# An own issue order for three pipeline slots, a last group mixed and stored in halves, and a swapped copy and shift, in a four-layer graph network

## The chip, the cores and the metric

One core of one Trainium2 chip runs the kernel. The time is device microseconds of one execution; lower is better. The kernel before has a median of 635.74 us over three runs (634.36 to 636.84).

## The reference

64 graphs of 128 nodes with 128 features pass through four layers. Each layer takes `h = relu(layernorm(x))` and adds its result to x:

```
x = x + attention(h, adj)        # 4 heads: leaky relu of e_i + e_j, masked by adj, softmax over neighbours
x = x + mlp((1 + eps) h + adj h) # 128 -> 256 -> 128, biases
x = x + adj (h W) + b            # graph convolution
x = x + gru(h, adj) * nodemask   # 5 steps: m = h W_l; agg = A^T m; h = gru_cell(agg, h)
```

All weights are inputs, and so are the biases, x, adj and the mask. The output is x, in float32.

## The kernel before, in words

Graphs are taken in groups of four (`GROUP`), so an operation has 512 columns on 128 partitions; there are 16 groups. Everything stays in SBUF from the first load to the last store. Five programs, one for each engine, are written out by hand; what orders them is the order of calls in each engine's `slot` function and semaphores between them.

**First layers.** `first_layers` runs a software pipeline of 19 slots. In slot `number`, `at(back)` is group `number - back`: the scores and softmax of `at(2)`, the attention product of `at(3)`, layer 1 of `at(4)`, layer 2 of `at(5)`, the layer norm ahead of the recurrent layer for `at(6)` and `at(7)`. The same functions are called in every slot, with exceptions for the first ones. The functions that matter here:

- Softmax of a group: TensorE adds the mask (`mask`) and the scores (`scores`) in four PSUM banks, ScalarE rectifies each graph's (`leaky`, L1132), VectorE takes the row maxima (`row_max`, L1327), GpSimd subtracts them (`less_max`, L720), ScalarE exponentiates (`exponential`, L1137), TensorE transposes (`turn_prob`, L878), and ScalarE and VectorE copy two graphs each to SBUF (`keep_probT`, L1142 and L1331).
- Attention: TensorE multiplies and sums (`attend`, `sum_up`), VectorE copies, divides and adds to x (`keep_attended`, `divide`, `add_attended`, L1354; signal `x_attended`). `mask` of graph 3 waits for `x_attended` of the group before, since it reuses its bank.
- Layer 1: VectorE computes `shift = -mean * rstd` (`shift_of`, L1302), ScalarE normalises (`normalise`, L1101), GpSimd adds (1 + eps) I to the transposed adjacency (`add_self`, L707), TensorE multiplies (`neighbours`, `hidden`, `out_0`).
- Layer 0: GpSimd centres and scales the next group (`centre`, L729; `scale`, L736), TensorE transposes it (`turn_y0`), ScalarE copies it (`keep_hT`, L1110). `centre` waits for the transpose of the group before.
- `GruWeights` fuses the five W_l with the input weights on TensorE (`turn`, `fuse`), copies the products on ScalarE (`keep`, `keep_fused`, L261) and derives a power-of-two scale from their largest magnitude on VectorE (`row_max` to `scaled_biases`). The recurrent layer first needs it in slot 18.

**Recurrent layer.** `gru_layer` takes 80 steps of four interleaved groups, with a tail in which pipeline slots 80 to 83 drain. For each step TensorE multiplies state parts and gathered parts by the gate weights (`gate`), ScalarE applies sigmoids and tanh (L1720, L1722, L1728, L1733), VectorE combines (L1779, L1788, L1792), GpSimd multiplies z by the state and adds the new state (L1745, L1751). A group that has ended is transposed back (`back`, L1668), masked and added to x (`finish`, L1766), and stored in one transfer (`store`, L1811).

Of the kernel before, what the change touches and what calls it, by code (L numbers as in the profile page):

```python
# [144 lines left out]
class GruWeights:  # L145
# [7 lines left out]
    def __init__(self, nc, io, t, psum, ctx, until_gru):  # L153
# [9 lines left out]
        self.fused_banks = [B_SUM, B_EDGE, B_SUM, B_EDGE, B_SUM]  # L163
# [48 lines left out]
    def turn(self, pe, lot):  # L212
# [5 lines left out]
        elif lot == 1:  # L218
            pe.wait_ge(self.wi_loaded, 16)
            pe.wait_ge(self.kept, 1)  # L220
            bank, sources = self.bank, [gw[:, 4, :], wi[:, 0, :], wi[:, 1, :], wi[:, 2, :]]
        elif lot == 2:
            pe.wait_ge(self.wh_loaded, 16)
            pe.wait_ge(self.kept, 2)
            bank, sources = self.bank, [wh[:, 0, :], wh[:, 1, :], wh[:, 2, :]]
# [9 lines left out]
    def keep(self, act, lot):  # L235
# [7 lines left out]
        elif lot == 2:  # L243
            last = a.copy(self.gf[:, GRU_STEPS, :], bank[:, 0:384])
# [4 lines left out]
    def fuse(self, pe, l):  # L249

        if l == 0:
            pe.wait_ge(self.kept, 3)
        elif l > 1:
            pe.wait_ge(self.fused_kept, l - 1)
# [15 lines left out]
    def all_rows_max(self, dve):  # L270

        dve.wait_ge(self.maxed, 3)
        self.nc.vector.tensor_reduce(self.top[:, 0:1], self.tops[:, :], AXIS.X, ALU.max).then_inc(self.maxed, 1)

    def turn_max(self, pe):
        pe.wait_ge(self.maxed, 4)
# [3 lines left out]
    def whole_max(self, dve):  # L280
# [3 lines left out]
        dve.wait_ge(self.maxed, 5)  # L284
        v.tensor_scalar(self.top1[:, 0:1], self.top1[:, 1:2], LEAST, None, ALU.max).then_inc(self.maxed, 1)

    def spread_max(self, pe):

        pe.wait_ge(self.maxed, 6)
# [187 lines left out]
LAYERS = range(4)  # L477

# [57 lines left out]
def first_layers(nc, io, t, psum, tiles, gru, score_weights, recurrent, ctx):  # L536
# [38 lines left out]
    shifted = sem("shifted")  # L575
    exp_done = sem("exp_done")
# [123 lines left out]
    def gpsimd(pool):  # L700
# [115 lines left out]
    def tensor(pe):  # L816
# [42 lines left out]
        def scores(group):  # L859

            pe.wait_ge(e_lo, group.count)
            for g in range(GROUP):
# [3 lines left out]
            for h in range(HEADS):  # L866
                for g in range(GROUP):
# [77 lines left out]
        def slot(at, number):  # L945
# [12 lines left out]
            if number == 4:  # L958
                pe.wait_ge(gru.fused_kept, 4)
            if at(2) and number > 2:  # L960
                score_terms(at(2))
            if number == 3:
                turn_adj(at(3))
            if at(3):
                attend(at(3), 1)
                sum_up(at(3))
            if number == 3:
                gru.turn(pe, 1)
            if number == 4:
                pe.wait_ge(gru.layers_loaded, gru.all_layers_loaded)  # L970
            if number == 5:
                pe.wait_ge(gru.kept, 4)
            if number == 7:
                pe.wait_ge(gru.maxed, 6)
            if number == 8:
                pe.wait_ge(gru.link, 2)
            if at(4):
                neighbours(at(4), 0, B_SUM, adjT1[at(4).odd], adjT1_ready,
                           (hid_ready[1], at(4).before(1)), (z_ready[0], at(4).before(1)))
            if at(3):  # L980
                turn_attended(at(3))
                turn_sums(at(3))
# [3 lines left out]
            if number == 3:  # L986
                gru.turn(pe, 2)
            if at(4):
# [3 lines left out]
            if at(2) and number > 2:  # L992
                mask(at(2), 2)
                mask(at(2), 3)
# [4 lines left out]
            if at(2):  # L999
                scores(at(2))  # L1000
            if at(5):
                neighbours(at(5), 1, B_EDGE, adjT[at(5).odd], adjT_ready,
                           (e_lo, at(5).before(-3)), (x_added[1], at(5).before(1)), (z_ready[1], at(5).before(1)))
            if number == 2:
                project(at(2))
                turn_y0(at(1))
                gru.turn(pe, 0)
            if number == 3:
                project(at(2))
                gru.fuse(pe, 0)  # L1010
                gru.fuse(pe, 1)
                gru.fuse(pe, 2)
            if number == 4:
                pe.wait_ge(hid_ready[1], 1)
                gru.fuse(pe, 4)
            if at(4):
                out_0(at(4))
            if number == 4:
                pe.wait_ge(gru.fused_kept, 5)
                gru.turn(pe, 3)  # L1020
            if number == 6:
                pe.wait_ge(hid_ready[1], 3)
                gru.turn_max(pe)
            if number == 7:
                pe.wait_ge(hid_ready[1], 4)
                gru.spread_max(pe)
# [6 lines left out]
            if number == 3:  # L1033
                turn_y0(at(1))
# [4 lines left out]
            if number == 3:  # L1039
                gru.fuse(pe, 3)  # L1040
            if at(1) and number > 3:
                turn_y0(at(1))
            if at(2):
                turn_prob(at(2), 2)
                turn_prob(at(2), 3)
            if number == 1:
# [38 lines left out]
    def scalar(act):  # L1085
# [49 lines left out]
        def exponential(group, g):  # L1135
            act.wait_ge(shifted, group.graph_count(g))
# [15 lines left out]
        def slot(at, number):  # L1152
            if number == 0:
                score_weights.pick_rows(act)
            if at(3) and number > 3:
# [12 lines left out]
            if at(2):  # L1168
                keep_e(at(2))
            if at(6):  # L1170
# [5 lines left out]
            if number == 3:  # L1176
                keep_adjT(at(3))
                gru.keep(act, 1)
                gru.keep(act, 2)
            if at(5):  # L1180
                normalise(at(5), 2)
            if at(4):
                keep_hidden(at(4), 0, B_TURN)
                keep_hidden(at(4), 1, B_SUM)
            if at(2):
# [3 lines left out]
                leaky(at(2), 3)  # L1189
            if at(5):  # L1190
                keep_z(at(5), 1, B_EDGE)
            if number == 2:
                keep_hT(at(1))
                gru.keep(act, 0)
            if number == 3:
                gru.keep_fused(act, 0)
                gru.keep_fused(act, 1)
            if number == 4:
                gru.keep_fused(act, 4)
            if at(3):  # L1200
# [5 lines left out]
            if at(2):  # L1206
                exponential(at(2), 0)
            if at(3) and number > 3:
                keep_adjT(at(3))
            if number == 2:  # L1210
                keep_hW(at(2))
            if at(2):
                exponential(at(2), 1)
            if number == 3:
                gru.keep_fused(act, 2)
            if number == 4:
                gru.keep(act, 3)
            if at(2) and number > 2:
                keep_probT(at(2), 0)
            if number == 3:  # L1220
                keep_hT(at(1))
# [5 lines left out]
            if at(1) and number > 3:  # L1227
# [42 lines left out]
    def vector(dve):  # L1270
# [57 lines left out]

        def keep_probT(group, g):
# [33 lines left out]
        def slot(at, number):  # L1363
            if number == 7:
                gru.whole_max(dve)
            if number == 8:
# [5 lines left out]
            if at(3):  # L1372
                keep_probT(at(3), 3)
# [4 lines left out]
            if at(2) and number > 2:  # L1378
                find_gone(at(2))
            if at(3):  # L1380
# [4 lines left out]
            if at(2):  # L1385
# [4 lines left out]
            if at(2):  # L1390
# [3 lines left out]
            if at(3):  # L1394
# [11 lines left out]
            if number == 8:  # L1406
# [3 lines left out]
            if number == 8:  # L1410
                gru.scale_bits(dve)
            if at(2):
                row_max(at(2), 3)
            if number == 4:
                gru.row_max(dve, 2, 4)
            if number == 5:
                gru.row_max(dve, 4, 6)
                gru.all_rows_max(dve)
            if number == 1:
# [3 lines left out]
                score_weights.scale(dve)  # L1423
            if at(4):
                add_out(at(4), 0, B_TURN)
            if number == 8:
                gru.scales(dve)
            if at(0):
                moments(at(0), 0, x_loaded[at(0).odd], at(0).loads)
            if number == 3:  # L1430
                gru.row_max(dve, 0, 2)
            if number == 0:
                score_weights.row_max(dve)
            if at(4) and number < 18:
                moments(at(4), 2, x_added[0], at(4).count)
            if number == 8:
                gru.scaled_biases(dve)
            if at(2):
                keep_probT(at(2), 1)
            if at(5):  # L1440
# [46 lines left out]
def gru_layer(nc, io, t, psum, first, weights, ctx):  # L1487
# [45 lines left out]
    out_ready = sem("out_ready")  # L1533
    stored = [sem(f"stored{s}") for s in range(STREAMS)]

    P = psum[:, :, :, :].rearrange("p s b c -> p (s b) c")
    R, Z, N, T, BACK = [0, 0], [2, 3], [1, 1], [7, 4], 5
    gb = t["gates_b"]
# [36 lines left out]

    def ended_before(j, back):
        return ended_at(j - back)
# [62 lines left out]
    def tensor(pe, remaining):  # L1640
# [30 lines left out]

        def slot(at, s, ended, j):
# [9 lines left out]
            if ended is not None:  # L1682
# [15 lines left out]
            remaining(j)  # L1698
            if here:
# [47 lines left out]

# [102 lines left out]
```

## Time and profile before

| what | us |
| --- | --- |
| median of 3 runs | 635.74 |
| lowest, highest | 634.36, 636.84 |
| the profiled execution | 636.28 |
| its span, first to last instruction | 634.4 |
| TensorE busy | 607.7 (96%) |
| ScalarE busy | 553.2 (87%) |
| VectorE busy | 525.4 (83%) |
| GpSimd busy | 402.3 (63%) |

The span is 1.88 us shorter than the execution it belongs to. Busy shares are averages over two stages with different work: the first layers up to about 260 us, the recurrent layer after them. TensorE's busy time is modelled for pipelined products. The mean granted TensorE clock was 0.995 of full speed.

### The profile page before, as it was taken

The numbers are of one execution on the slowest core, as the hardware profiler recorded it, in microseconds if no ns is written. First come the engines' busy times: TensorE is split into PE (matmuls) and PEld (weight loads), VectorE is DVE, ScalarE is ACT, GpSimd is POOL, SyncE is SP. The second block draws the span as 40 slices with busy tenths as digits, with TensorE's granted clock in tenths as the row PEclk, the third lists the DMA queues.
The fourth block names the chain that finished last, engine by engine and source line by source line (L and its number), as shares of the span: only waits on it lengthen the run. The fifth ranks groups of instructions, "written<-read, shape, count | busy, mean of one in ns | idle before, by whom it ended". The sixth has DMA issues, their size and how long they took to land. (4 is left out here: it accounts for less than half of the span.)

```text
span 634.4 us, 14614 instructions
## 1 busy us (share of the span) xinstructions
PE 607.7 (96%) x5070; PEld 387.2 (61%) x5070; DVE 525.4 (83%) x1312; ACT 553.2 (87%) x1042; POOL 402.3 (63%) x361
## 2 busy tenths in 40 slices
PE   5899999999999999999999999999999999999994
PEld 3567778788888887556545455555555555554552
DVE  6678898988888888889979888888788787787875
ACT  4688899999999999787988888898988889888883
POOL 3456777778877877367577656555565655555564
PEclk9999999999999999999999999999999999999998
DMA  8101011111100000224322324334243423335332
GB/s 182 49 4 54 18 48 32 52 40 33 52 20 18 19 19 1 51 51 62 57 50 51 67 51 85 71 78 80 56 83 67 84 56 80 67 68 84 70 81 67
DMA packets 113643, 35.79 MB, mean 56 GB/s; under 512 B 86625, under 2 KB 113570, under 8 KB 113570
## 3 DMA queue, kind: packets, MB, share of 16 engines
q1 hardware_dynamic: 113424, 34.79, 26.4%
q8 instruction: 41, 0.67, 0.4%
q14 instruction: 32, 0.26, 0.1%
q10 hardware_dynamic: 146, 0.07, 0.0%
HBM read 9.67 MB, written 4.19 MB: 22 GB/s over the span
## 5 line engine op out<-in xcount | busy, mean ns | idle before, releaser
L53 PE MATMUL psum<-h_parts,gru_w 128*128 128x512 f16 x720 | 182.5, 379 | 1.0 <-DVE r L1792 0.8
L53 PE MATMUL psum<-t_parts,gru_w 128*128 128x512 f16 x720 | 181.5, 379 | 0.0
L1751 POOL TENSOR_TENSOR h0T<-r,zh 128x512 f32<-128x512 f32 x80 | 101.6, 1270 | 107.2 <-DVE r L1788 107.1
L1745 POOL TENSOR_TENSOR zh<-z,h0T 128x512 f32<-128x512 f32 x80 | 103.9, 1299 | 34.2 <-ACT z L1720 33.8
L53 PEld LDWEIGHTS psum<-h_parts,gru_w 128*128 128x128 f16 x720 | 69.8, 98 | 82.7 <-DVE r L1792 4.2
L53 PEld LDWEIGHTS psum<-t_parts,gru_w 128*128 128x128 f16 x720 | 66.8, 98 | 66.5 <-DVE t_parts L1775 1.7
L1633 DVE TENSOR_TENSOR h_parts<-h0T,h_parts 128x512 f16<-128x512 f32 x80 | 65.1, 813 | 38.9 <-ACT h_parts L1620 38.7
L1717 ACT CAST t_parts<-psum 128x512 f16<-128x512 f32 x80 | 46.8, 585 | 35.8 <-PE psum L53 35.8
L720 POOL TENSOR_TENSOR prob<-prob,row_max 128x512 f32<-128x512 f32 x64 | 64.5, 1040 | 10.9 <-DVE row_max L1327 10.4
L1775 DVE TENSOR_TENSOR t_parts<-psum,t_parts 128x512 f16<-128x512 f32 x80 | 55.1, 689 | 18.9 <-ACT t_parts L1717 16.6
L1720 ACT ACTIVATE z<-psum,gates_b 128x512 f32<-128x512 f32 x80 | 62.2, 778 | 5.7 <-PE psum L53 0.9
L1728 ACT ACTIVATE r<-r,gates_b 128x512 f32<-128x512 f32 x80 | 65.5, 819 | 0.1
L1792 DVE SCALAR_TENSOR_TENSOR r<-psum,gates_b,r 128x512 f32<-128x512 f32 x80 | 59.8, 747 | 4.4 <-ACT r L1733 4.3
L1733 ACT ACTIVATE r<-psum,gates_b 128x512 f32<-128x512 f32 x80 | 61.6, 770 | 1.7 <-PE psum L53 1.7
L1788 DVE TENSOR_TENSOR r<-r,zc 128x512 f32<-128x512 f32 x80 | 60.1, 751 | 2.8 <-ACT r L1728 2.7
L729 POOL TENSOR_TENSOR y<-x_all,mean_var 128x512 f32<-128x512 f32 x31 | 33.3, 1076 | 44.6 <-DVE mean_var L1285 27.6
L1722 ACT ACTIVATE zc<-psum,gates_b 128x512 f32<-128x512 f32 x80 | 61.5, 769 | 0.0
L1101 ACT ACTIVATE y<-x_all,shift,rstd 128x128 f32<-128x128 f32 x128 | 52.7, 488 | 5.1 <-DVE shift L1302 5.1
L1277 DVE BATCH_NORM_STATS2 stats<-x_all 128x6 f32<-128x128 f32 x256 | 54.9, 276 | 1.9 <-DMA x_all<-in_x 1.5
L53 PEld LDWEIGHTS psum<-edges,h_nodes 128*128 128x128 f16 x640 | 42.3, 98 | 20.7 <-issue 2.3
L1779 DVE TENSOR_TENSOR r<-psum,r 128x512 f32<-128x512 f32 x80 | 54.4, 680 | 0.0
L714 POOL TENSOR_TENSOR x_all<-x_all,b 128x512 f32<-128x512 f32 x32 | 40.7, 1273 | 17.2 <-ACT y L1101 14.7
(148 smaller groups left out, 1126.1 us busy)
## 6 DMA issues: line engine op xcount, KB each, us to landing
x_all<-in_x SPq DMA_DIRECT2D x16, 256.0 KB, 3.8
adj<-in_adj SPq DMA_DIRECT2D x16, 256.0 KB, 3.0
out_x<-y SPq DMA_DIRECT2D x14, 256.0 KB, 2.5
h_nodes<-h_parts SPq DMA_TRANSPOSE x80, 3.1
out_x<-zT SPq DMA_DIRECT2D x2, 256.0 KB, 2.3
gw<-in_L_gnn_weight SPq DMA_DIRECT2D x1, 320.0 KB, 5.4
W<-in_L_gnn_W SPq DMA_DIRECT2D x2, 128.0 KB, 3.1
wi<-in_L_gnn_w_ih SPq DMA_DIRECT2D x1, 192.0 KB, 5.5
```

What stands on the lines that cost most here:

```text
L53: return nc.tensor.matmul(out, lhsT, rhs, start=start, stop=stop)
L720: pool.tensor_tensor(prob[:, g, :, :], prob[:, g, :, :], top[:, g, :].unsqueeze(2).to_broadcast([128, HEADS, NODES]), ALU.subtract).then_i ...
L1633: v.tensor_tensor(by_graph(hp[now.s][:, 1, :]), state(now), by_graph(hp[now.s][:, 0, :]), ALU.subtract)\
L1720: a.activation(z[one.s][:, :], one.Z, ACT.Sigmoid, bias=col(B_Z), scale=col(UNSCALE))\
L1722: a.activation(zc[one.s][:, :], one.Z, ACT.Sigmoid, bias=col(B_NZ), scale=col(N_UNSCALE))\
L1728: a.activation(r[one.s][:, :], r[one.s][:, :], ACT.Tanh, bias=col(B_IN), scale=col(UNSCALE))\
L1733: a.activation(r[here.s][:, :], here.R, ACT.Sigmoid, bias=col(B_R), scale=col(UNSCALE))\
L1745: pool.tensor_tensor(by_graph(zh[now.s][:, :]), by_graph(z[now.s][:, :]), state(now), ALU.mult)\
L1751: pool.tensor_tensor(state(now), by_graph(r[now.s][:, :]), by_graph(zh[now.s][:, :]), ALU.add)\
L1775: v.tensor_tensor(tp[one.s][:, 1, :], one.T, tp[one.s][:, 0, :], ALU.subtract).then_inc(t_lo, 1)
L1788: v.tensor_tensor(r[two.s][:, :], r[two.s][:, :], zc[two.s][:, :], ALU.mult).then_inc(mixed, 1)
L1792: v.scalar_tensor_tensor(r[one.s][:, :], one.N, col(B_HN), r[one.s][:, :], ALU.add, ALU.mult)\
```

## The change

1. **Slots 2 to 4 get an order of their own**, on TensorE, ScalarE, VectorE and GpSimd. In slot 3 the scores of graphs 0 to 2 stand ahead of the mask of graph 3; edges and layer-1 statistics of VectorE stand behind the row maxima; the adjacency transpose of group 0 moves from slot 3 to slot 2. For groups 0 and 1 VectorE subtracts the row maxima of the last graph (`less_last`), which GpSimd did. In slot 4 the hidden-layer copies stand among the exponentials, and some copies and the transpose of the next group stand later. `keep_hT(group 3)` and `rstd_of(group 1, 1)` move into slot 5.
2. **The recurrent weights are prepared over more slots**: fusing in slots 3 to 6, row maxima one step each in slots 5 to 10, scale in slots 11 to 13. Some banks change.
3. **Every slot from 4 on**: VectorE copies the last transposed probabilities (`keep_probT(at(3), 3)`) ahead of `shift_of(at(4), 1)`, not behind it.
4. **The end**: in slots 80 to 83 `back` stands behind the gate products, `finish` and `store` of an ended group one slot later. The last group's state is mixed by VectorE in two halves, transposed in two banks, finished and stored as two transfers.

The diff, cut to its core:

```diff
# first layers, GpSimd
-            if at(4):
+            if at(4) and number > 4:
                 add_self(at(4))
+            if number == 4:
+                centre(at(1), 0)
...
+            if number == 3:
+                add_self(at(3))
             if at(2):
                 less_max(at(2), 0)
                 less_max(at(2), 1)
                 less_max(at(2), 2)
+            if at(2) and number > 3:
                 less_max(at(2), 3)
-            if at(0) and number > 0:
+            if at(0) and number > 0 and number < 3:
+                centre(at(0), 0)
+            if at(0) and number > 3:
                 centre(at(0), 0)
# first layers, TensorE
...
+            if number == 3:
+                scores(at(2), 0, GROUP - 1)
+            if at(2) and number > 2:
                 mask(at(2), 3)
...
+            if number == 3:
+                scores(at(2), GROUP - 1, GROUP)
+            if at(2) and number > 3:
                 scores(at(2))
...
+            if number == 4:
+                hidden(at(4), 0, B_TURN, (hT_ready, at(2)))
+                hidden(at(4), 1, B_SUM)
...
+            if number == 5:
+                pe.wait_ge(hid_ready[1], 2)
+                gru.fuse(pe, 3)
             if number == 6:
                 pe.wait_ge(hid_ready[1], 3)
-                gru.turn_max(pe)
+                gru.fuse(pe, 4)
...
+            if number == 11:
+                pe.wait_ge(hid_ready[1], 8)
+                gru.turn_max(pe)
# first layers, ScalarE
...
+            if number == 5:
+                rstd_of(at(4), 1)
+                keep_hT(at(2))
+                gru.keep_fused(act, 2)
             if number == 4:
-                gru.keep_fused(act, 3)
+                gru.keep(act, 2)
+                gru.keep_fused(act, 0)
...
-            if at(4):
+            if at(4) and number > 4:
                 keep_hidden(at(4), 0, B_TURN)
                 keep_hidden(at(4), 1, B_SUM)
...
+            if number == 4:
+                keep_hidden(at(4), 0, B_TURN)
...
+            if number == 4:
+                keep_hidden(at(4), 1, B_SUM)
             if at(2):
                 exponential(at(2), 1)
...
+            if number == 5:
+                gru.keep_fused(act, 3)
+            if number == 6:
+                gru.keep_fused(act, 4)
+            if number == 7:
                 gru.keep(act, 3)
...
+            if number == 4:
+                gru.keep_fused(act, 1)
# first layers, VectorE
+        def less_last(group):
+
+            g = GROUP - 1
+            dve.wait_ge(max_done, group.graph_count(g))
+            v.tensor_tensor(prob[:, g, :, :], prob[:, g, :, :],
+                            top[:, g, :].unsqueeze(2).to_broadcast([128, HEADS, NODES]),
+                            ALU.subtract).then_inc(last_shifted, 1)
...
+            if at(3):
+                keep_probT(at(3), 3)
             if at(4):
                 shift_of(at(4), 1)
-            if at(3):
-                keep_probT(at(3), 3)
...
+            if number == 3:
+                less_last(at(2))
+                find_edges(at(2))
+                moments(at(3), 1, x_attended, at(3).count)
...
             if number == 5:
-                gru.row_max(dve, 4, 6)
+                gru.row_max(dve, 0, 1)
+            if number == 6:
+                gru.row_max(dve, 1, 2)
...
+            if number == 10:
+                gru.row_max(dve, 5, 6)
                 gru.all_rows_max(dve)
# recurrent layer, TensorE
-            if ended is not None:
+            if ended is not None and j < SLOTS * ROUNDS:
                 back(ended)
...
             remaining(j)
+            if j == SLOTS * ROUNDS + STREAMS - 1:
+                last_back()
+            elif j >= SLOTS * ROUNDS:
+                back(ended)
# recurrent layer, VectorE
+        def last_mix(two):
+
+            dve.wait_ge(cand_ready, two.count)
+            dve.wait_ge(zc_ready, two.count)
+            dve.wait_ge(zh_ready, two.count)
+            half = GROUP // 2
+            for k in range(2):
+                cols = slice(k * half * NODES, (k + 1) * half * NODES)
+                v.tensor_tensor(r[two.s][:, cols], r[two.s][:, cols], zc[two.s][:, cols], ALU.mult).then_inc(half_mixed, 1)
+                dve.wait_ge(half_mixed, k + 1)
+                v.tensor_tensor(t["h0T"][:, bass.ds(two.graph + k * half, half), :],
+                                r[two.s][:, cols].rearrange("p (g n) -> p g n", g=half),
+                                zh[two.s][:, cols].rearrange("p (g n) -> p g n", g=half), ALU.add).then_inc(half_ready, 1)
# recurrent layer, SyncE
-            if ended is not None and ended.count > GROUPS - STREAMS:
-                store(ended)
+            if j == SLOTS * ROUNDS + STREAMS - 1:
+                last, half = last_ended(), GROUP // 2
+                for k in range(2):
+                    sp.wait_ge(half_out, k + 1)
+                    sp.dma_start(io["out"][bass.ds(last.first + k * half, half)].rearrange("g n d -> n g d"),
+                                 out[last.buffer][:, k * half:(k + 1) * half, :]).then_inc(stored[last.buffer], 16)
```

`last_back` waits for the first half, transposes two graphs into bank 6, then waits for the second half and for the `out_ready` of the group before and transposes two into bank 5. `last_finish` on VectorE follows it half by half.

## Rows read from the trace of the kernel before

**Rows 1.** Windows: start:end and length, then busy time of each engine.
```profile
core 0: us, PE busy (x) PEld busy (x) DVE busy (x) ACT busy (x) POOL busy (x), PEclk, DMA share, GB/s
13.22:27.94 14.72, 12.20 (x145) 9.29 (x145) 9.37 (x27) 9.41 (x21) 7.15 (x8) 1.00 0.30 62
27.94:42.95 15.01, 13.81 (x150) 8.99 (x150) 11.00 (x35) 12.45 (x28) 8.57 (x8) 1.00 0.01 2
42.95:58.60 15.65, 14.20 (x165) 10.64 (x165) 13.59 (x44) 13.70 (x33) 8.51 (x8) 1.00 0.19 52
58.60:74.47 15.87, 14.63 (x178) 11.86 (x178) 14.20 (x54) 14.19 (x36) 11.84 (x12) 1.00 0.06 19
105.61:121.49 15.88, 14.93 (x182) 12.25 (x182) 14.32 (x59) 14.67 (x37) 11.85 (x12) 1.00 0.18 52
121.49:136.18 14.69, 14.69 (x182) 12.32 (x182) 13.10 (x52) 14.55 (x37) 11.86 (x12) 1.00 0.07 20
136.18:150.86 14.68, 14.68 (x182) 12.30 (x182) 13.09 (x52) 14.54 (x36) 11.86 (x12) 1.00 0.19 55
209.95:224.63 14.68, 14.68 (x182) 12.31 (x182) 13.10 (x52) 14.54 (x36) 11.64 (x12) 1.00 0.08 20
400.00:500.00 100.00, 100.00 (x609) 52.06 (x607) 80.57 (x130) 88.77 (x137) 57.39 (x46) 1.00 0.37 73
```

**Rows 2.** Waits of ScalarE from 58.6 to 224.63: total, times, longest.
```profile
ACT y L1101 <- DVE shift L1302: 3.0, 3, 1.0
```

**Rows 3.** Timeline, 127.6 to 129.5: start, us, instruction [idle before].
```profile
127.71 1.04 PE L878 MATMUL psum<-ident,prob 128*128 128x128 f32 x8
...
128.05 1.04 POOL L729 TENSOR_TENSOR y<-x_all,mean_var 128x512 f32<-128x512 f32 x1 [1.14 <-PE psum L819]
...
128.97 0.15 DVE L1302 SCALAR_TENSOR_TENSOR shift<-mean_var,rstd 128x4 f32<-128x4 f32 x1
129.04 0.68 DVE L1331 COPY probT<-psum 128x512 f32<-128x512 f32 x1
129.05 1.29 POOL L707 TENSOR_TENSOR adjT<-adjT,self_eye 128x512 f32<-128x512 f32 x1
...
129.34 0.52 ACT L1101 ACTIVATE y<-x_all,shift,rstd 128x128 f32<-128x128 f32 x1
```

**Rows 4.** Timeline, 113.0 to 114.8, the boundary one slot earlier.
```profile
113.17 1.28 POOL L707 TENSOR_TENSOR adjT<-adjT,self_eye 128x512 f32<-128x512 f32 x1
...
113.58 0.90 DVE L1302 SCALAR_TENSOR_TENSOR shift<-mean_var,rstd 128x4 f32<-128x4 f32 x1
...
114.60 0.49 ACT L1101 ACTIVATE y<-x_all,shift,rstd 128x128 f32<-128x128 f32 x1 [1.01 <-DVE shift L1302]
```

**Rows 5.** Timeline of slots 3 to 5: mask, statistics, rectification, normalisation.
```profile
26.97 0.10 PEld L53 LDWEIGHTS psum<-gone,identb 128*128 128x128 bf16 x1 [1.18 <-DVE x_all L1354]
...
27.94 2.06 ACT L1132 ACTIVATE prob<-psum 128x512 f32<-128x512 f32 x4 [1.46 <-PE psum L53]
28.17 0.38 DVE L1285 BATCH_NORM_AGGREGATE mean_var<-stats 128x2 f32<-128x6 f32 x4
...
29.33 1.04 POOL L720 TENSOR_TENSOR prob<-prob,row_max 128x512 f32<-128x512 f32 x1 [5.46 <-DVE row_max L1327]
...
41.12 0.69 ACT L1150 ACTIVATE hid<-psum,b 128x512 f32<-128x512 f32 x1 [0.82 <-PE psum L53]
...
42.95 2.06 ACT L1132 ACTIVATE prob<-psum 128x512 f32<-128x512 f32 x4 [0.28 <-PE psum L53]
44.88 0.51 ACT L261 COPY gf<-psum 128x384 f32<-128x384 f32 x1
...
51.71 0.49 ACT L1101 ACTIVATE y<-x_all,shift,rstd 128x128 f32<-128x128 f32 x1 [0.86 <-DVE shift L1302]
```

**Rows 6.** Timeline, 624 to the end.
```profile
624.50 1.11 DVE L1766 SCALAR_TENSOR_TENSOR y<-psum,mask,x_all 128x128 f32<-128x128 f32 x4
...
625.54 0.68 DVE L1779 TENSOR_TENSOR r<-psum,r 128x512 f32<-128x512 f32 x1
...
626.25 0.81 ACT L1728 ACTIVATE r<-r,gates_b 128x512 f32<-128x512 f32 x1
627.10 0.69 DVE L1788 TENSOR_TENSOR r<-r,zc 128x512 f32<-128x512 f32 x1 [0.88 <-ACT r L1728]
...
627.99 1.26 POOL L1751 TENSOR_TENSOR h0T<-r,zh 128x512 f32<-128x512 f32 x1 [1.10 <-DVE r L1788]
...
630.47 1.12 DVE L1766 SCALAR_TENSOR_TENSOR zT<-psum,mask,x_all 128x128 f32<-128x128 f32 x4 [1.64 <-PE psum L1668]
```

More of the change, by code:

```diff
@@ L243, in keep @@
         elif lot == 2:
-            last = a.copy(self.gf[:, GRU_STEPS, :], bank[:, 0:384])
+            last = a.copy(self.gf[:, GRU_STEPS, :], P[:, B_EDGE, 0:384])
         else:
@@ L857, in mask, with scores @@
                gone[group.odd][:, g, :].unsqueeze(1).to_broadcast([128, HEADS, NODES]), True, False)
-        def scores(group):
+        def scores(group, first=0, end=GROUP):
             pe.wait_ge(e_lo, group.count)
-            for g in range(GROUP):
+            for g in range(first, end):
                 rows = slice(g * ROWS, (g + 1) * ROWS)
@@ L866, in scores @@
             for h in range(HEADS):
-                for g in range(GROUP):
+                for g in range(first, end):
                     rows = slice(g * ROWS, (g + 1) * ROWS)
@@ L985, in slot @@
                 mask(at(2), 1)
-            if number == 3:
-                gru.turn(pe, 2)
-            if at(4):
+            if number == 4:
+                neighbours(at(4), 0, B_SUM, adjT1[at(4).odd], adjT1_ready)
+            if at(4) and number > 4:
                 hidden(at(4), 0, B_TURN,
@@ L1154, in slot @@
                 score_weights.pick_rows(act)
-            if at(3) and number > 3:
+            if at(3) and number > 4:
                 keep_hW(at(3))
@@ L1384, in slot @@
                 shift_of(at(5), 2)
-            if at(2):
+            if at(2) and number > 3:
                 keep_e_lo(at(2))
@@ L1670, in back, with last_back @@
             last.then_inc(back_psum, 1)
+        def last_back():
+            last, half = last_ended(), GROUP // 2
+            for k, bank in enumerate(HALF_BANKS):
+                pe.wait_ge(half_ready, k + 1)
+                if bank == BACK:
+                    pe.wait_ge(out_ready, last.count - 1)
+                for g in range(half):
+                    done = nc.tensor.transpose(P[:, bank, g * 128:(g + 1) * 128],
+                                               t["h0T"][:, last.first + k * half + g, :], t["ident"][:, :])
+                done.then_inc(half_back, 1)
         def slot(at, s, ended, j):
@@ L1769, in finish, with last_finish @@
             last.then_inc(out_ready, 1)
+        def last_mix(two):
[10 more added lines that the diff above has]
+                                zh[two.s][:, cols].rearrange("p (g n) -> p g n", g=half), ALU.add).then_inc(half_ready, 1)
+        def last_finish():
+            last, half = last_ended(), GROUP // 2
+            for k, bank in enumerate(HALF_BANKS):
+                dve.wait_ge(half_back, k + 1)
+                for g in range(half):
+                    n = k * half + g
+                    done = v.scalar_tensor_tensor(out[last.buffer][:, n, :], P[:, bank, g * 128:(g + 1) * 128],
+                                                  t["mask"][:, bass.ds(last.first + n, 1)],
+                                                  t["x"][:, last.first + n, :], ALU.mult, ALU.add)
+                done.then_inc(half_out, 1)
         def slot(at, s, ended, j):
@@ L1784, in slot @@
                 state_parts(dve, now)
-            if two:
+            if two and two.count == SLOTS * ROUNDS:
+                last_mix(two)
+            elif two:
                 dve.wait_ge(cand_ready, two.count)
```

210 lines of the change are left out of this document (132 added, 78 removed).

## The prediction

> **What bounds the kernel now.** I read the page for the span and engine shares, then the busy time in windows cut from one leaky rectification to the next (one window per group in the first layers), then the waits of ScalarE, then the timeline of one slot boundary, of the first three groups and of the end. Of the 634.4 us span, the first layers fill about 260 us and the recurrent layer the rest. In the recurrent layer TensorE does not pause (100 us busy of 100 from 400 on) [rows 1], so whatever is lost or won in the first layers moves it as a block and stays in the time.
>
> In the first layers ScalarE sets the pace: from 121.49 on a group takes 14.68 us with 14.55 us of ScalarE work in it, that is, no gap [rows 1]. Some slots take 15.9 us with the same work, and the three waits of 1.0 us for the small shift explain them [rows 1, 2]. The boundary shows why. The shift of layer 1 (four numbers per partition, both inputs in SBUF) takes 0.15 us where it falls just ahead of GpSimd's `adjT1` addition, and 0.90 us where it arrives during that addition: it then ends at 114.48, and the addition at 114.45 [rows 3, 4]. ScalarE's normalisation cannot begin before it.
>
> The three windows ahead of that hold 45.38 us with 35.56 us of ScalarE work: 9.8 us of idle time is the ceiling of what an own order for the first groups can recover [rows 1].
>
> **The swap of copy and shift.** It applies to every slot from 4 on. In an unstalled slot VectorE reaches the pair at 128.97. Today shift first: it ends 129.12, GpSimd starts the addition at 129.05, ScalarE normalises from 129.34 with no gap. After the swap the copy comes first (0.68 us, reading PSUM, which runs beside the addition unhindered), so the shift arrives at about 129.6, inside the addition of 129.05 to 130.34 [rows 3]. By the stalled boundary it ends 0.03 us after the addition and ScalarE starts 0.12 us later [rows 4]: 130.48 in place of 129.34, a gap of 1.14 us. ScalarE has no slack elsewhere, so the slot becomes 14.68 + 1.14 = 15.82 us, just what the stalled slots take now.
>
> The addition cannot easily get out of the way: it follows GpSimd's centring, and that follows TensorE's transpose of the next group, which stands in the same place of the order. TensorE gains a little: the last probabilities are copied 0.4 to 0.8 us earlier relative to the normalisation, so its next products wait on the normalisation, not on the sums. By my walk that brings the centring and the addition 0.14 us forward. I take 1.05 us per slot, between 0.52 (if the shift were only delayed by its new place: copy end 129.72 + 0.15 against 129.34) and 1.14.
>
> The unstalled slots pay and the stalled ones do not gain. Between the rectifications at 58.60 and 224.63 lie eleven slots, 166.03 us [rows 1]. Changed: 11 x 15.73, less 0.48 for the first, which has no copy of h0T yet (14.19 us of work against 14.67) = 172.6. Difference **+6.5 us**. The last two boundaries have the addition out of the way; there the shift is late by the copy alone, 0.27 and at most 0.6 us, part of it hidden in the thinning queue: **+0.5**.
>
> The Trainium skill (SBUF — State Buffer, "Who interferes with whom") says that a VectorE instruction with two SBUF inputs and a GpSimd instruction that reads SBUF block each other for a whole instruction, and that issue order decides who waits; it speaks against this swap. By that rule a slot pays 1.14 less what TensorE brings, without it 0.52; the trace agrees with the rule, by the common end at 114.45.
>
> **The first three groups.** Three edits shorten the chain of slot 3. The scores of three graphs no longer wait for the fourth's mask, which today stands 1.18 us for `x_attended` [rows 5]; edges and layer-1 statistics (0.42 + 0.86 + 0.38 us) move behind the row maxima; the subtraction for the last graph goes from GpSimd (1.04 us, fourth in line) to VectorE. That subtraction has two SBUF inputs, so I let it wait out GpSimd's and save nothing by it. Walking each engine's queue, the rectification of slot 3 starts at 26.5 rather than 27.94, that of slot 4 at 41.1 rather than 42.95 [rows 5]. From there ScalarE works without a gap, but more is queued: rectification 2.06, hidden 2 x 0.6, exponentials 2.8, adjT 0.6, two probability copies 1.2, two fused-weight copies 1.0, hW 0.6, hT 0.6, rstd 0.5, less the overlap of neighbours, some 10.2 us. The normalisation of slot 5 then begins at 51.3, against 51.71 now [rows 5]: **-0.4 us**. Most of the 1.8 us went into hidden-layer and transposed copies that today lie ahead of the rectification. The bounds: -4 (less than half the idle time recovered) and +1.
>
> **Weights of the recurrent layer.** Fusing, copying and scaling are spread over slots 4 to 13. Three ScalarE copies (two of 0.5, one of 0.2 us) fall into slots 5 to 7. They stand ahead of the boundary whose gap is set by GpSimd, so the 1.05 us gap covers them: 0. Without that cover they cost 1.2 in all. Six row maxima of about 0.47 us on VectorE in slots 5 to 10 delay the shift, but it still ends with the addition: 0. The scale steps of slots 12 and 13 add 0.4 us ahead of the copy, inside the same wait: 0. The factors are needed at the split of slot 18, five slots later. Adjacency loads are issued earlier for group 2, and never awaited: 0.
>
> **The end.** Today VectorE finishes the group before (1.11 us at 624.50) ahead of the last sum at 625.54, and the transposes stand before the last gate product [rows 6]. Both move back, so z comes about 0.4 us earlier, the last tanh starts near 625.65 instead of 626.25. But the half-wise mix also waits for `zh` on GpSimd, which I get at 626.75, so the product starts about 0.35 us earlier than 627.10. Four half operations (about 0.42 each, from 0.69 for a whole, with a semaphore between) end near 628.7; GpSimd's 1.26 us and its hand-over vanish (end now 629.25). Then VectorE finishes group 14 (1.12 us) first, since that now comes a slot later, and the last half needs the bank it frees: the last output row is ready at 631.2 against 631.6, and its store is half as large. **-0.5 us**, between -1.2 and +0.3. Store issues go from one to two of 0.4 us on SP; the first is covered by the second half's work.
>
> **Sum.** 6.5 + 0.5 - 0.4 - 0.5 = +6.1 us. The profiled execution took 636.28 us, 1.88 us around its span, so 642.4; against the median of 635.74 that is **641.8 us**, +1.0%. Bounds of this case: 3.2 below (first groups at -4, others small) and 2.5 above, 638.5 to 644.5.
>
> **Rivals.**
> *Order without a lock.* The four-number shift is delayed by its place only, 0.52 us a slot: 11 x 15.20 - 0.48 = 166.7, +0.7; with +0.5, -0.4 and -0.5 the time is 636.0. Against it: the end at 114.48 beside 114.45, and 0.15 us when free. Chance 0.10.
> *The shift finds the gap* (the other side). If GpSimd's addition began at least 0.55 us later than VectorE now allows, or the copy ended before 129.09, the shift would slip in between centring and addition in every slot, and the five stalls of today would vanish: eleven slots at 14.68 less 0.48 = 161.0, -5.0; with -0.4 and -0.5 it is 629.8. For it: it happens today in most slots. Against: TensorE's last probability transposes end at 128.75, so the copy cannot end before about 129.6. It could also go this side if the own order recovered 9 us, more than nine tenths of the idle time. Chance 0.07.
> *A second late shift.* The layer-2 shift could arrive behind the centring of layer 3 and wait out the bias addition (1.27 us), holding the low score parts and so the rectification by some 0.4 us a slot: 641.8 + 4.4 = 646.2. By my walk it arrives 0.3 us before that point. Chance 0.08.
> The forecast keeps 0.75.
>
> **Range and chances.** 635.5 to 645.0 takes in the lockless case and leaves out the gap case and the second late shift, 0.15 together, and the edge of the forecast. Over and under 0.5% (3.2 us), about what a measurement here can tell from no change, the cases give faster 0.07, same 0.12 (lockless, and the forecast with a ramp gain above 4), slower 0.81.
>
> **What would show it.** Right: shifts of layer 1 in slots 5 to 16 that end with the `adjT` addition, ScalarE waiting about 1.0 us for each, eleven rectifications 15.6 to 15.9 us apart, the first three windows about as long as now, the last output a few tenths nearer to the last gate product. Wrong: intervals of 14.7 us with shifts of 0.15 us; a rectification of slot 4 before 39 us; or a pace set by another wait than the shift. The step most likely to be off is the walk through the first groups, the only one with no row of its own for the new order.

## The result and the profile after

| | median us | ratio to before | 95% interval |
| --- | --- | --- | --- |
| before | 636.13 (4 runs beside it) | | |
| changed | 641.48 (4 runs) | 1.009 | 1.0075 to 1.0104 |

The change makes the kernel slower by 5.35 us against the four runs beside it (0.8%), and by 5.74 us against the 635.74 from which the forecast was made (0.9%). The ratio in the table agrees with the second. The profiled execution of the changed kernel took 641.24 us with a span of 639.4; the span grew by 5.0 us. The forecast was 641.8 us.

The windows of the changed kernel, cut from rectification to rectification (columns as in [rows 1]):

```profile
12.52:24.43 11.91, 9.86 (x135) 7.27 (x135) 9.64 (x23) 8.94 (x19) 8.26 (x8) 1.00 0.32 78
24.43:37.98 13.55, 11.84 (x149) 8.17 (x149) 11.38 (x33) 10.57 (x25) 6.07 (x6) 1.00 0.01 2
37.98:56.21 18.23, 16.40 (x170) 11.42 (x170) 14.38 (x48) 15.37 (x35) 9.46 (x9) 1.00 0.16 45
56.21:72.42 16.21, 14.98 (x180) 12.23 (x180) 14.29 (x53) 14.54 (x36) 11.85 (x12) 1.00 0.06 18
...
120.38:136.02 15.64, 15.08 (x182) 12.20 (x182) 13.81 (x53) 14.51 (x36) 11.84 (x12) 1.00 0.07 19
...
167.48:183.59 16.11, 15.28 (x184) 12.60 (x184) 14.17 (x54) 14.66 (x36) 12.02 (x12) 1.00 0.18 51
...
214.89:230.54 15.65, 14.85 (x182) 12.27 (x182) 13.82 (x53) 14.52 (x36) 11.85 (x12) 1.00 0.07 19
```

Read them against [rows 1]. A window runs from the rectification of one slot to that of the next; it is called that slot's interval below, and the one that begins at 56.21 is slot 5's. ScalarE works 14.5 us in a slot as before, but most slots take 15.65 us where the kernel before took 14.68. Slots 5, 6, 7 and 12 take more: 16.21, 16.30, 16.01 and 16.11. The three windows of the first groups are shorter, then longer: 11.9 and 13.6 for 14.7 and 15.0, then 18.2 for 15.7, and the rectification of slot 5 starts at 56.21 instead of 58.60. The waits of ScalarE from there to slot 16:

```profile
ACT y L1138 <- DVE shift L1356: 10.9, 11, 1.0
```

Eleven boundaries, eleven waits of about 1.0 us, where [rows 2] shows three. One boundary in the timeline (start, us, instruction):

```profile
127.94 1.27 POOL L710 TENSOR_TENSOR adjT<-adjT,self_eye 128x512 f32<-128x512 f32 x1
...
128.32 0.68 DVE L1393 COPY probT<-psum 128x512 f32<-128x512 f32 x1
...
128.92 0.32 DVE L1356 SCALAR_TENSOR_TENSOR shift<-mean_var,rstd 128x4 f32<-128x4 f32 x1
...
129.36 0.88 ACT L1138 ACTIVATE y<-x_all,shift,rstd 128x128 f32<-128x128 f32 x2 [1.00 <-DVE shift L1356]
```

The last copy of the probabilities runs at its usual 0.68 us inside GpSimd's addition. The shift behind it ends at 129.24, 0.03 us after the addition's 129.21: the same distance as at the stalled boundary of [rows 4]. All eleven shifts from slot 5 to slot 15 end within 0.06 us of the end of the addition beside them. A duration of 0.32 us looks harmless, but ScalarE has by then waited 1.00 us: the shift is short because it arrives late in the addition, and late because the copy stands ahead of it.

The end of the changed kernel:

```profile
632.98 0.43 DVE L1901 TENSOR_TENSOR r<-r,zc 128x256 f32<-128x256 f32 x1 [0.33 <-POOL zh L1865]
...
634.23 0.42 DVE L1903 TENSOR_TENSOR h0T<-r,zh 128x256 f32<-128x256 f32 x1
634.57 1.12 DVE L1888 SCALAR_TENSOR_TENSOR zT<-psum,mask,x_all 128x128 f32<-128x128 f32 x4
635.61 1.29 DVE L1913 SCALAR_TENSOR_TENSOR zT<-psum,mask,x_all 128x128 f32<-128x128 f32 x4
...
635.84 0.41 PE L1784 MATMUL psum<-ident,h0T 128*128 128x128 f32 x2 [1.49 <-DVE zT L1888]
```

The `DVE` row at 634.57 is the finish of the group before, the one at 635.61 that of the last group. The recurrent layer runs 6.40 us later than before (one of its state additions starts at 611.25 before and at 617.65 after). Moved by that, the last row of [rows 6] would end at 637.99; it ends at 636.90, 1.1 us nearer. From there to the end of the span it is 2.5 us in place of 2.8. As the prediction had it, the product waits for `zh` (0.33 us) and the last transposes wait for the finish of the group before.

### The profile page after: what moved, and what is told of

The parts are those of the page before. It is cut to its first block and busy times, and to the rows that moved or that the text cites. A ratio compares the mean times of both kernels' runs of the same rounds, so it can differ in the third digit from the quotient of the medians.

```text
span 639.4 us, 14622 instructions
## 1 busy us (share of the span) xinstructions
PE 608.8 (95%) x5070; PEld 384.8 (60%) x5070; DVE 533.0 (83%) x1320; ACT 553.0 (86%) x1042; POOL 400.0 (63%) x358
## 5 line engine op out<-in xcount | busy, mean ns | idle before, releaser
L1873 POOL TENSOR_TENSOR h0T<-r,zh 128x512 f32<-128x512 f32 x79 | 100.3, 1270 | 106.9 <-DVE r L1937 106.8
L1138 ACT ACTIVATE y<-x_all,shift,rstd 128x128 f32<-128x128 f32 x128 | 52.6, 482 | 13.8 <-DVE shift L1356 13.6
```

What stands on the lines that cost most here:

```text
L1873: pool.tensor_tensor(state(now), by_graph(r[now.s][:, :]), by_graph(zh[now.s][:, :]), ALU.add)\
```

## The experiments

All times are medians, and each ratio is taken against runs of the kernel before beside it on the same chip. The changed kernel was not run again beside them: a difference to it sets its 641.48 against a run whose own kernel before had a median of 635.69 or 635.36, where the changed kernel's had 636.13. Such differences are uncertain by about what lies between these medians, 0.4 to 0.8 us, so lengths from the traces are given with the main ones.

**The swap alone.** The kernel before with this and nothing else:

```diff
+            if at(3):
+                keep_probT(at(3), 3)
             if at(4):
                 shift_of(at(4), 1)
-            if at(3):
-                keep_probT(at(3), 3)
```

> The kernel before with the swap and nothing else. Blocked by GpSimd's adjT1 addition (theory 1): the eleven intervals between the rectifications of slots 5 and 16 take 15.65 us each, less 0.48 for the first, so 171.7 against 166.0; with 0.5 from the last two boundaries the time is 636.1 + 6.2 = 642.3 us. Delayed by its place alone (theory 2): a gap of 0.5 us a slot, 166.7 in all, 636.8 to 637.3 us. Order of no weight: 636.1 us.

Measured: 642.66 us against 635.69, ratio 1.0114 (1.0097 to 1.0131). From slot 5 to slot 16 the rectifications take 173.1 us (57.61 to 230.72) against 166.0. Two of its windows, columns as before:

```profile
121.13:136.78 15.65, 14.85 (x182) 12.27 (x182) 13.82 (x52) 14.52 (x36) 11.87 (x12) 1.00 0.06 18
215.05:230.72 15.67, 14.87 (x182) 12.28 (x182) 13.84 (x53) 14.53 (x37) 11.88 (x12) 1.00 0.07 19
```

The swap by itself costs +7.0 us, more than the whole change. The place alone would have given about 637. The late slots take the expected 15.65 us. The 1.4 us by which 173.1 exceeds the expected 171.7 lie in slots 5 to 7, which take 15.99, 15.76 and 16.12.

**The swap undone** in the changed kernel, all else kept (the same four lines the other way).

> The changed kernel with the shift ahead of the copy again, all else kept. Theory 1: the slots from 8 on go back to 14.7 us where the shift meets the gap ahead of the addition; slots 5 to 7 keep their extra copies and some stalled ones stay, as in the kernel before. 634 to 636 us, about 6 below 641.5. Theory 2: 641.0 less about 1, near 640.

Measured: 636.61 us against 635.69, 1.0017 (1.0007 to 1.0026): 4.9 us under the changed kernel. Two kinds of slots follow each other in its windows:

```profile
102.27:118.14 15.87, 14.90 (x182) 12.24 (x182) 14.33 (x53) 14.67 (x36) 11.86 (x12) 1.00 0.18 51
118.14:134.02 15.88, 14.92 (x182) 12.25 (x182) 14.34 (x53) 14.69 (x37) 11.87 (x12) 1.00 0.07 19
...
181.13:197.01 15.88, 14.94 (x182) 12.25 (x182) 14.34 (x59) 14.67 (x36) 11.73 (x12) 1.00 0.07 19
197.01:211.69 14.68, 14.68 (x182) 12.31 (x182) 13.09 (x52) 14.54 (x36) 11.87 (x12) 1.00 0.07 20
```

Its waits of ScalarE in the same stretch:

```profile
ACT y L1138 <- DVE shift L1356: 5.0, 5, 1.0
```

With the shift first, a boundary is either won (the shift slips in ahead of the addition, 14.68) or lost (it falls inside, 15.88). Five of the eleven slots are lost here, four of them in a row from 102.27 to 165.86, against three in the kernel before; only the last two take 14.68, and the others 15.1 to 15.4 without a wait for the shift. The eleven take 170.0 us, so this run takes back 4.4 of the changed kernel's 174.3 and not all of its excess of 8.3. The expectation of slots near 14.7 from slot 8 on failed, though the total came within 1 us.

The two kinds of slots do not hold the same work. Every lost slot, here (8 to 11 and 13) and in the kernel before (5, 6 and 8), is one in which VectorE also carries a step of the recurrent weights, a row maximum or a scale step: mostly 53 to 59 instructions where the slots of 14.68 have 52. Behind the last such step (slot 13 here, slot 8 there) no slot is lost. Some slots with a step are not lost, and no run moved these steps alone with the shift first, so that they make the shift miss the gap fits the traces but is not shown.

**The new end alone.** The kernel before with the changed kernel's recurrent layer:

> The kernel before with the recurrent layer of the changed one (late transposes, last group in halves) and nothing else. From the two traces (last gate product to last row 1.1 us nearer, store 0.3 us shorter): 636.1 - 1.4 = 634.7 us. By the prediction's term of -0.5: 635.6 us. The windows ahead of 620 us are as in the kernel before.

Measured: 634.48 us against 635.69, 0.9981 (0.9970 to 0.9992), that is -1.2 us. The windows of the first layers agree with the kernel before within 0.05 us from slot 3 on. The prediction's -0.5 was too small.

**The addition taken out of the way.** The changed kernel, swap and all, with one GpSimd instruction moved:

```diff
-            if at(4) and number > 4:
-                add_self(at(4))
...
+            if at(3) and number > 3 and number < 18:
+                add_self(at(3))
             if at(0) and number > 3:
                 centre(at(0), 0)
```

> The changed kernel with one GpSimd instruction moved: from slot 4 on the adjT1 addition of a group stands at the end of the slot before, ahead of the centring of the next group, in GpSimd's idle time. VectorE's order is that of the changed kernel, swap included. Theory 1 (the addition blocks the shift): the shift of layer 1 takes 0.15 to 0.3 us in every slot, the gap of ScalarE falls from 1.0 to about 0.5 us (what the copy's place costs), 641.5 - 5.5 = 636 us. Theory 2 (only the place in VectorE's queue counts): the gap stays 1.0 us, 641.5 us.

Measured: 636.57 us, 1.0019 (1.001 to 1.0028), 4.9 us under the changed kernel; slots 5 to 15 take 169.4 us in place of 174.3, the same 4.9. VectorE's program is the same as there, so the 4.9 us are what GpSimd's addition at this place costs. A late boundary in its timeline:

```profile
218.52 0.68 DVE L1393 COPY probT<-psum 128x512 f32<-128x512 f32 x1
...
219.12 0.15 DVE L1356 SCALAR_TENSOR_TENSOR shift<-mean_var,rstd 128x4 f32<-128x4 f32 x1
...
219.39 1.26 ACT L1138 ACTIVATE y<-x_all,shift,rstd 128x128 f32<-128x128 f32 x3 [0.37 <-DVE shift L1356]
```

The shift is back at 0.15 us, and ScalarE's gap is 0.37 us: that is what the copy's place costs once the blocking is gone. Its windows, an early slot and a late one:

```profile
118.67:134.15 15.48, 15.08 (x182) 12.21 (x182) 13.65 (x53) 14.52 (x37) 11.81 (x12) 1.00 0.07 20
211.04:226.06 15.02, 14.86 (x182) 12.28 (x182) 13.19 (x53) 14.53 (x37) 11.82 (x12) 1.00 0.07 20
```

In slots 14 and 15 the 15.65 falls to 15.02. Slots 5 to 13 stay at 15.3 to 15.7: there VectorE also carries a step of the weights, in slots 5 to 10 a row maximum of 0.54 us, which the long addition had covered.

**Both: addition ahead, swap undone.**

> The changed kernel with both edits: the addition ahead of the centring, as in the run before, and the shift ahead of the copy again. Theory 1: the shift now meets only the end of the centring and has no copy ahead of it; ScalarE's gap falls from 0.8 to 0.1 to 0.3 us, intervals near 14.8 to 15.0 us in place of 15.5, so 636.6 - 6 = 630.5 us. Theory 2: as the undone swap alone, 636.6 us.

Measured: 632.50 us, 0.9951 (0.9935 to 0.9967), 3 us faster than the kernel before. The late slots take 14.7 us, those from 5 to 13 15.0 to 15.4, so it missed 630.5 by 2.0. The waits of ScalarE from slot 5 to slot 16:

```profile
ACT y L1138 <- DVE shift L1356: 1.2, 4, 0.4
```

**The weights behind the transposes.** The changed kernel; on TensorE the last two fusing products and the mask's transpose move, on ScalarE their copies:

```diff
-            if number == 5:
-                pe.wait_ge(hid_ready[1], 2)
-                gru.fuse(pe, 3)
...
             if number == 4:
                 turn_y0(at(1))
                 gru.fuse(pe, 2)
+            if number == 5:
+                gru.fuse(pe, 3)
```

> The changed kernel with the last two fusing products and the node mask's transpose (slots 5 to 7) behind the probability transposes on TensorE, and their ScalarE copies behind the last copy of the slot. Theory A (the products of TensorE, ahead of the transpose that releases the centring, carry GpSimd's addition back, so the copies are not covered by the wait): the intervals 16.21, 16.30 and 16.01 fall to 15.7 each, 641.5 - 1.5 = 640.0 us. Theory B (the ScalarE copies alone lengthen these slots): nothing changes, 641.5 us.

Measured: 640.24 us, 1.0078 (1.0066 to 1.0090), against the changed kernel's 641.48 and 1.009 (1.0075 to 1.0104). By the medians it is 1.2 us less, but the intervals of the ratios overlap; the windows are the firmer evidence. The three intervals fall from 16.21, 16.30 and 16.01 to 16.01, 16.01 and 15.65, which is 0.85 us, and the later ones stay. Theory A gave 1.5 and is borne out by direction. The part that stays in slots 5 and 6 comes with a new wait: ScalarE stands 0.9 us in each for the late fusing product. The timeline of TensorE in the changed kernel shows the mechanism (same columns as above):

```profile
58.90 0.81 PE L53 MATMUL psum<-wiT,gwT 128*128 128x384 f32 x2
...
62.64 0.60 PE L829 MATMUL psum<-ident,y 128*128 128x128 f32 x4
```

The transpose that releases the centring starts 6.43 us after the rectification at 56.21. In [rows 3]'s slot it starts at 127.27, 5.78 us after 121.49: 0.65 us later here, behind the fusing product, and GpSimd's addition with it. The same holds slot by slot: this transpose starts 6.43 us after the rectification in slot 6, 6.13 in slot 7, 5.89 in slot 11, 6.24 in slot 12 and 5.78 in the ordinary ones, and the interval is 9.9 us longer than that in each.

**The shift in the slot before.** The changed kernel with

```diff
-            if at(4):
+            if at(4) and number in (4, 5):
                 shift_of(at(4), 1)
...
+            if at(3) and 4 < number < 18:
+                shift_of(at(3), 1)
             if at(2) and number < 4:
                 keep_probT(at(2), 1)
```

> The changed kernel with the shift of layer 1 taken out of the boundary: from slot 5 on it is computed late in the slot before, ahead of the second copy of probabilities, where GpSimd waits for TensorE. If the late shift is the whole cost of the rhythm (theory 1 carried through), ScalarE has no gap at the boundary and the intervals are 14.7 us from slot 8 on and 15.2 ahead of it: 641.5 less 11.5 = 630 us. If another wait stands close behind (the last copy of probabilities, TensorE's products), a gap stays and the time is above 634 us.

Measured: 635.88 us, 1.0009 (1.0000 to 1.0017). Intervals of 15.8 us remain in slots 8 to 10 and 13, again slots with a step of the weights on VectorE. The wait had only moved, as its timeline shows:

```profile
124.75 1.04 POOL L732 TENSOR_TENSOR y<-x_all,mean_var 128x512 f32<-128x512 f32 x1 [1.14 <-PE psum L829]
124.95 0.86 DVE L1356 SCALAR_TENSOR_TENSOR shift<-mean_var,rstd 128x4 f32<-128x4 f32 x1
...
125.73 0.68 DVE L1393 COPY probT<-psum 128x512 f32<-128x512 f32 x1
...
126.52 0.65 PE L53 MATMUL psum<-probT,hW 128*32 128x128 f32 x16 [0.54 <-DVE probT L1393]
```

ScalarE no longer waits for the shift, but the shift met GpSimd's centring (both end at 125.8) and held up the copy behind it, which TensorE's attention product awaits. My expectation had looked at ScalarE alone.

**The shift in the slot before and the weights behind.**

> The two edits of the two runs before together: the shift in the slot before, and the weights' TensorE and ScalarE work of slots 5 to 7 behind the slot's own. With no gap left, ScalarE's copies of 0.5, 0.5 and 0.2 us are on the path wherever they stand, so against the shift's edit alone at most 0.5 us is won: 629.5 us.

Measured: 637.25 us, 1.0029 (1.0018 to 1.0040): 1.4 us slower than the run before it. Without the gap the late copies are paid: slots 5 to 7 take 2.0 us more than in the run before it, and ScalarE waits 1.8 us for the late fusing products. What helped under the stall hurts without it.

**The kernel before with the addition ahead and the new end.** Its own order of the first groups, its own places for the weights, shift ahead of the copy.

> The kernel before (its order of the first groups, its places for the weights, shift ahead of the copy) with the addition ahead of the centring and the new end. If what is left of the gaps in the run with both edits (15.1 us in slots 6 to 13) comes from the weights spread over slots 5 to 13, the intervals here are 14.7 to 15.0 us from slot 6 on, the rectification of slot 16 at 221 us or earlier, and the time is 636.1 - 4.5 - 1.2 = 630.4 us. If the own order of the first groups is what makes the other kernel good, this one is above 632.5 us.

Measured: 632.24 us, 0.9948 (0.9932 to 0.9963), the fastest of this study. Slot 16 is rectified at 221.04 (before: 224.63), in a profiled execution that was itself 1.1 us under the median. It missed 630.4 by 1.8. Its slots 5 to 8 take 15.71, 15.14, 15.15 and 15.13 us, the slots behind them 14.7 (14.9 in two). The last of the slow ones and the first of the others:

```profile
102.59:117.72 15.13, 14.93 (x182) 12.24 (x182) 13.58 (x59) 14.67 (x36) 11.82 (x12) 1.00 0.19 55
117.72:132.42 14.70, 14.70 (x182) 12.28 (x182) 13.15 (x52) 14.55 (x36) 11.81 (x12) 1.00 0.07 20
```

The step from 15.1 to 14.7 comes where the weights' work ends. This kernel's own steps run up to slot 8, the last at 109.24; the expectation had left them out. In the run with both edits they run up to slot 13, and that is where its 15.0 to 15.4 end. So the first alternative of the expectation is borne out: but for the two of 14.9, which the kernel before has too, the slots above 14.7 are those with the weights' steps.

The median equals that of the run with both edits (632.50) within its spread, so the own order of the first groups and the spreading of the weights together bring nothing that can be measured here. The traces show two parts that work against each other: slots 5 to 15 take 166.2 us there and 164.5 here, and slot 5 begins at 55.81 there and at 56.59 here.

## Why the prediction was right

The sign and the mechanism of the main term were right. That the total came so close (641.8 for 641.48) was in part luck: two terms were 1.8 us too low together, two others 2.9 us too high, and they cancelled for the most part.

| term | predicted | profiled execution, or run |
| --- | --- | --- |
| swap, slots 5 to 16 | +6.5 | +7.1 (swap alone: 173.1 less 166.0) |
| weights in slots 5 to 13 | 0 | +1.2 (174.3 less 173.1; moving three steps gave 0.85 back in slots 5 to 7) |
| last two boundaries | +0.5 | +0.5 (6.40 less 8.30 less -2.39) |
| first three groups | -0.4 | -2.4 (58.60 to 56.21); -1.4 against the swap alone (57.61) |
| end | -0.5 | -1.4 by trace, -1.2 in the run of the end alone |
| sum | +6.1 | +5.0 of span, +5.35 of median |

- **The boundary.** A gap of 1.05 us was predicted, and 0.9 to 1.04 was measured at eleven boundaries. That GpSimd's addition blocks the shift is shown, not argued: the same VectorE program with the addition elsewhere is 4.9 us faster, and the shift returns to 0.15 us. The lockless rival (636.0) falls by the same run and by the swap alone. Its price per slot was right in kind: 0.52 was predicted for the place alone, 0.34 to 0.37 was measured in the late slots.
- **Rule and trace.** The Trainium skill's rule (SBUF — State Buffer, "Who interferes with whom") spoke against the swap: two SBUF inputs on VectorE and a GpSimd instruction that reads SBUF exclude each other for a whole instruction. The trace agrees: common ends within 0.03 us at [rows 4] and at the changed kernel's boundary, and within 0.02 us in the run with the shift in the slot before, with the centring in place of the addition.
- **The shift finds the gap** (629.8) did not happen with copy first. The same gap is what the kernel before lives on, and the run with the swap undone shows how thin it is: three lost slots became five. The prediction speaks here of "the five stalls of today"; [rows 2] has three. They and slot 7, which takes 15.15 us without any wait for the shift, make up most of its 5.0 us.
- **A second late shift** did not appear; that shift stayed at 0.32 us in most slots.
- **The weights, the first mis-sized term.** The step "They stand ahead of the boundary whose gap is set by GpSimd, so the 1.05 us gap covers them: 0" overlooked that their TensorE products stand ahead of the transpose that releases GpSimd. The cover moved along with what it should cover. The intervals 16.21, 16.30 and 16.01 are 0.56, 0.65 and 0.36 above the 15.65 of the ordinary slots (the swap alone has 0.34, 0.11 and 0.47 there, by its own weights' steps). The step "inside the same wait: 0" for the scale failed in the same way: slot 12 takes 16.11, 0.46 too much, and its transpose starts 0.46 us late. The kernel before pays as much for it in slot 7 (15.15 for 14.68), so this part does not enter the difference. That VectorE's row maxima cost nothing under the wait held: slots 8 and 9 carry one and take 15.65. With the addition out of the way the slots with one take 15.48 against 15.02, about 0.5 more.
- **The first groups, the second.** The rectification of slot 4 was forecast at 41.1 and came at 37.98, that of slot 3 at 26.5 and came at 24.43. Of the latter, 0.7 us lies ahead of it: slot 2 begins at 12.52 for 13.22, 12.5 to 13.3 in the other runs, so this part is scatter of the first loads. The step that failed is the walk from queue to queue. One link can be read: the prediction let the last graph's subtraction on VectorE wait out GpSimd's "and save nothing by it". The subtractions of slot 3, first in the kernel before, then in the changed one:

```profile
29.33 4.03 POOL L720 TENSOR_TENSOR prob<-prob,row_max 128x512 f32<-128x512 f32 x4 [5.46 <-DVE row_max L1327]
```

```profile
25.83 3.48 POOL L723 TENSOR_TENSOR prob<-prob,row_max 128x512 f32<-128x512 f32 x3 [1.75 <-DVE row_max L1381]
27.56 0.85 DVE L1387 TENSOR_TENSOR prob<-prob,row_max 128x512 f32<-128x512 f32 x1
```

  Before, the fourth subtraction ended 5.42 us after the rectification of slot 3; in the changed kernel VectorE's ended 3.98 us after it and GpSimd's third 4.88. How much of the term this link explains was not tried apart. The prediction's signs failed here: the rectification of slot 4 came before 39 us, which it had named as a sign of being wrong, and the first three windows were not about as long as now. The rest of the gain was given back as forecast, 18.2 us in slot 4 to 5, by the copies that were put off. How much of the 2.4 us the order itself brings is not settled. Kernels with the old order reached slot 3 at 27.94, 27.93, 26.97 and 26.66, though none of them has an edit ahead of it, so the profiled executions scatter by more than a microsecond here; those with the new order reached it at 24.4 to 25.1, and slot 5 at 55.8 to 56.8. The last run, without the new order, reaches slot 5 at 56.59: from slot 4 on, where the addition has moved, it is 0.7 us quicker than the kernel before.
- **The end.** The prediction's chain was right link by link; the four half operations took 1.67 us instead of about 1.9, began 0.5 us earlier than before where about 0.35 was forecast, and the shorter store brought 0.3.
- **What sets the pace.** The prediction says that ScalarE sets it. In the slots of 14.68 us [rows 1] ScalarE is busy for 14.55, but TensorE's modelled busy time is 14.68, the whole slot. In slot 7 of the kernel before TensorE is again busy throughout, and ScalarE has half a microsecond to spare:

```profile
90.46:105.61 15.15, 15.15 (x184) 12.64 (x184) 13.62 (x54) 14.68 (x37) 11.86 (x12) 1.00 0.06 19
```

  The gaps at the boundary are ScalarE's, as shown; which of the two engines sets the pace where there is no gap was not tried.

## What to carry to other kernels

Before two instructions of VectorE change places, look at what GpSimd does at that moment. Here an instruction with two SBUF inputs and four elements per partition took 0.15 us when free and up to 0.95 us when it met a GpSimd addition, while a PSUM copy kept its 0.68 us inside the same addition. Where a slot is bound by one engine without slack, a small instruction at its boundary sets the rhythm of every slot; the cheap remedy was to move GpSimd's instruction into its own idle time (632.2 us, 0.9948 of before, of which the new end alone brings 1.2 us), not to reorder VectorE. When a stall is counted as cover for new work, check that no part of that work sits in the chain that ends the stall.

## What the runs showed that I had not expected

- With the shift first, a slot takes 14.68 us or, when the boundary is lost, 15.88; the kernel before loses three of eleven, the run with the swap undone five, four of them in a row. All of them are slots in which VectorE carries a step of the recurrent weights. So a small piece of unrelated work on an engine with idle time may be what loses 1.2 us at the boundary; it was not tried by itself. That run also differs from the kernel before in the first groups, and the two were not told apart.
- A blocked instruction hides in a list of durations: the shifts of the changed kernel took 0.15 to 0.95 us, 0.32 at the boundary shown, against 0.90 in [rows 4]; yet ScalarE waited about 1.0 us for each. The wait, not the duration, is the thing to read.
